# Registers in the middle of each chunk of keys, and 156 score columns for the maxima instead of 228

## What is computed

```python
x = x + attention(group_norm(x))      # 12 heads of 32, window 7 x 7 on a canvas of 48 x 48
x = x + expert_mlp(group_norm(x))     # 4 experts, the best 2 of them

# attention, for every query pixel q of an image and every head:
k_cat = concat([k, reg_k]); v_cat = concat([v, reg_v])   # 48*48 pixels and 16 registers
scores = (q . k_cat) / sqrt(32)
scores = where(in the 7 x 7 window around q (clipped to the canvas) or a register, scores, -1e30)
o = softmax(scores) @ v_cat
```

## Time and profile before

| what | us |
|---|---|
| median of 3 runs | 680.63 |
| lowest and highest | 676.43, 681.11 |
| the profiled execution, its own time | 682.01 |
| its span in the trace | 680.2 |

### The profile page before, as it was taken

One profiled execution on the slowest core, in us unless ns is written; L12 is line 12 of the kernel. 1 busy time (PEld: TensorE's weight loads), 2 busy tenths in 40 slices (PEclk: granted clock), 3 DMA queues, 4 the chain that ended last, 5 costly groups with the idle time before them and its releaser, 6 DMA issues.

```text
span 680.2 us, 22432 instructions
## 1 busy us (share of the span) xinstructions
PE 591.2 (87%) x9235; PEld 413.0 (61%) x9235; DVE 475.6 (70%) x1030; ACT 303.2 (45%) x598; POOL 285.0 (42%) x425
## 2 busy tenths in 40 slices
PE   3578778999799987998899988988878888997997
PEld 2336656677666766567675766757656454564554
DVE  4786465788787889876667868876798875772332
ACT  0663345314554277513562255441774527544231
POOL 4106588235232564436892452224646112212231
PEclk9979689999999999999999999998998998997999
DMA  8959584797419952398518954199530010110112
GB/s 296 177 128 279 168 215 123 192 238 204 118 31 232 274 152 73 84 237 235 145 51 199 250 175 136 37 248 242 164 92 22 1 36 35 56 51 35 71 44 97
DMA packets 131806, 95.94 MB, mean 141 GB/s; under 512 B 67437, under 2 KB 125481, under 8 KB 131705
## 3 DMA queue, kind: packets, MB, share of 16 engines
q1 hardware_dynamic: 121960, 75.18, 43.3%
q0 software_dynamic: 9744, 19.33, 9.1%
HBM read 58.11 MB, written 35.54 MB: 138 GB/s over the span
## 4 chain that ended last, share of the span: by engine, by line
PE 51%; DVE 17%; DMA 11%; SPq 9%; ACT 5%; issue 5%; POOL 2%; ACTq 0%; DVEq 0%; POOLq 0%
PE ps L1041 38%; SPq L270 6%; DVE MX L549 5%; PE ps L1200 4%; DMA KB<-kscr 4%; PE ps L1151 4%; DMA WR<-in_wqkv 2%; DMA vscr<-VT 2%; PE ps L1177 2%; DVE GT_ L481 2%; ACT XH L807 1%; SPq L253 1%; DMA VR<-vscr 1%; DVE SUMT L562 1%; DMA kscr<-KT 1%
## 5 line engine op out<-in xcount | busy, mean ns | idle before, releaser
L549 DVE TENSOR_REDUCE MX<-ps 128x2 f32<-128x456 f32 x216 | 125.4, 626 | 56.4 <-PE ps L1151 55.4
L1041 PE MATMUL ps<-XH,WQ 128*128 128x384 f16 x810 | 146.5, 337 | 9.3 <-DVE XH L491 8.0
L1041 PEld LDWEIGHTS ps<-XH,WQ 128*128 128x128 f16 x810 | 79.8, 101 | 68.2 <-issue 15.2
L866 ACT ACTIVATE PT<-ps 128x448 f32<-128x448 f32 (+1 forms) x162 | 78.7, 511 | 62.6 <-PE ps L1177 62.0
L1151 PE MATMUL ps<-KB,QS 120*32 120x228 f16 x1728 | 66.2, 270 | 29.9 <-DMA KB<-kscr 11.9
L425 POOL TENSOR_TENSOR KT<-QS,KT 128x384 f16<-128x384 f32 x36 | 32.7, 919 | 110.1 <-ACT KT L955 110.1
L1177 PE MATMUL ps<-QS,KB 122*128 122x112 f16 (+1 forms) x864 | 64.5, 215 | 10.2 <-ACT PT L866 5.6
L1041 PE MATMUL ps<-WQ,XH 128*128 128x128 f16 x972 | 63.2, 224 | 2.6 <-issue 2.1
L372 POOL DMA_DIRECT2D QS<-MT x72 | 38.2, 534 | 63.9 <-ACT MT L856 63.8
L1200 PE MATMUL ps<-PT,VR 128*32 128x112 f32 (+1 forms) x1296 | 61.1, 262 | 2.8 <-DMA VR<-vscr 2.8
L1151 PEld LDWEIGHTS ps<-KB,QS 120*32 120x32 f16 x1728 | 34.6, 97 | 47.4 <-DVE MX L549 17.4
(11 more groups left out here) (169 smaller groups left out, 1010.0 us busy)
## 6 DMA issues: line engine op xcount, KB each, us to landing
KB<-kscr SPq DMA_DIRECT2D x108, 192.0 KB, 7.5
kscr<-KT SPq DMA_DIRECT2D x72, 192.0 KB, 2.5
VR<-vscr SPq DMA_DIRECT2D x216, 56.0 KB
QS<-qscr SPq DMA_DIRECT2D x108, 96.0 KB, 6.8
out<-X SPq DMA_DIRECT2D x12, 576.0 KB, 3.3
X<-in_x SPq DMA_DIRECT2D x6, 576.0 KB, 8.2
qscr<-QT POOLq DMA_DIRECT2D x18, 192.0 KB, 3.5
qscr<-PT POOLq DMA_DIRECT2D x18, 192.0 KB, 5.1
```

The source lines that it names most:

```text
L549: V.tensor_reduce(out=MX[:, s % 2, t, 2 * pair:2 * pair + 2], in_=ps[:, S_BANK(s, i), 0:2 * RUN].rearrange("p (h n) -> p h n", h=2), op=AL ...
L866: A(PTS[n % 4][:, 0:w], ps[:, ST_BANK(n), 0:w], ACT.Exp, scale=SCORE).then_inc(s_["exd"], 1)
L1041: last = mm(bank, lhsT(a, k), rhs(b, k), start=(k == 0 and n == 0), stop=(finish and k == steps - 1 and n == 2))
```

## The change

The 16 registers move from the end of each chunk to its middle: 4 rows of keys (56 columns), 16 registers, 4 rows of keys. A run of 32 queries then needs three rows ahead, four rows, three rows behind and one block of registers, whichever half of the chunk its queries belong to: 42 + 56 + 16 + 42 = 156 columns, starting at the chunk or 56 columns into it. What follows from it:

- the copy of keys into chunks writes two halves of 4 rows with a gap of 16 columns (one more dimension in the access pattern);
- a chunk's values no longer lie on 112 partitions in a row but on 56 and 56 with the registers' 16 between, so each chunk is loaded by two DMAs of 4 rows of pixels;
- the wait ahead of a tile's values is split: the first three chunks wait for the first three steps of tile s - 2 only;
- the key tables follow the new order, the slot keeps its 868 columns, and the matmuls on zeros become 36 of 168 columns.

```diff
-LEAD, TAIL = 3 * KW + REGS, 3 * KW
-SLOTW = LEAD + STRIPS * CHUNK + TAIL
-RUN = LEAD + CHUNK + TAIL
+HALO = 3 * KW
+HALF = 4 * KW
+SLOTW = 2 * HALO + STRIPS * CHUNK + REGS
+RUN = 2 * HALO + HALF + REGS
...
-WARM = 26
+WARM = 36
...
-            return bass.AP(flat.tensor, flat.offset, [list(flat.ap[0]), [CT_, TILES], [PADW, 8], [1, KW]])
+            return bass.AP(flat.tensor, flat.offset, [list(flat.ap[0]), [CT_, TILES], [4 * PADW, 2], [PADW, 4], [1, KW]])
...
-                if 36 * gi + 6 * (s - 1) > 0:
-                    sp.wait_ge(s_["pv"], 36 * gi + 6 * (s - 1))
                 if gi == 0 and s == 0:
                     sp.wait_ge(s_["vpad"], 32)
                 for a in range(STRIPS):
-                    sp.dma_start(VR[0:8 * KW, s % 2, a, :], vscr[8 * a:8 * a + 8, CT_ * s:CT_ * s + KW, :]).then_inc(vr_in[s % 2][a // 3], 16)
+                    if a % 3 == 0:
+                        if 36 * gi + 6 * (s - 2) + a + 3 > 0:
+                            sp.wait_ge(s_["pv"], 36 * gi + 6 * (s - 2) + a + 3)
+                    for half in range(2):
+                        sp.dma_start(VR[half * (HALF + REGS):half * (HALF + REGS) + HALF, s % 2, a, :],
+                                     vscr[8 * a + 4 * half:8 * a + 4 * half + 4, CT_ * s:CT_ * s + KW, :]).then_inc(vr_in[s % 2][a // 3], 16)
...
                 for part in range(2):
-                    last = V.tensor_copy(KT[:, a % 3, part, :, 0:8 * KW].rearrange("p s (r c) -> p s r c", c=KW), windows(a, part))
+                    to = KT[:, a % 3, part, :, :]
+                    parts = bass.AP(to.tensor, to.offset, [list(to.ap[0]), [CHUNK, TILES], [HALF + REGS, 2], [KW, 4], [1, KW]])
+                    last = V.tensor_copy(parts, windows(a, part))
...
                     for j in range(4):
-                        a, q0 = 2 * t + j // 2, s * SN + 128 * t + 32 * j
+                        at, q0 = CHUNK * (2 * t + j // 2) + j % 2 * HALF, s * SN + 128 * t + 32 * j
                         last = mm(ps[32 * j:32 * j + 32, S_BANK(s, i), hh * RUN:(hh + 1) * RUN], QS[0:SROWS, h, q0:q0 + 32],
-                                  KB[0:SROWS, h, slot(s), CHUNK * a:CHUNK * a + RUN], start=True, stop=True)
+                                  KB[0:SROWS, h, slot(s), at:at + RUN], start=True, stop=True)
```

More of the change, by code:

```diff
@@ L252, in keys_in @@
                 for j, part in enumerate((0, 1, 0)):
-                    sp.dma_start(KB[DH * j:DH * (j + 1), :, slot(s), LEAD:LEAD + STRIPS * CHUNK],
+                    sp.dma_start(KB[DH * j:DH * (j + 1), :, slot(s), HALO:HALO + STRIPS * CHUNK],
                                  kscr[part, :, s, :, :].rearrange("(h d) a n -> d h (a n)", d=DH)).then_inc(kb_in[slot(s)], 16)
@@ L327, in _ @@
             nc.gpsimd.memset(KU[:, :, :, :, W + 3:PADW], 0.0).then_inc(s_["pads"], 1)
-            nc.gpsimd.memset(KB[0:96, :, :, 0:LEAD], 0.0).then_inc(s_["pads"], 1)
-            nc.gpsimd.memset(KB[0:96, :, :, SLOTW - TAIL:SLOTW], 0.0).then_inc(s_["pads"], 1)
+            nc.gpsimd.memset(KB[0:96, :, :, 0:HALO], 0.0).then_inc(s_["pads"], 1)
+            nc.gpsimd.memset(KB[0:96, :, :, HALO + STRIPS * CHUNK:SLOTW], 0.0).then_inc(s_["pads"], 1)
             def low_half(n, blk, k):
@@ L342, in register_keys @@
                     for part in range(2):
-                        last = nc.gpsimd.tensor_copy(KT[:, i, part, :, CHUNK - REGS:CHUNK],
+                        last = nc.gpsimd.tensor_copy(KT[:, i, part, :, HALF:HALF + REGS],
                                                      KR[:, part, gi % KC, :].unsqueeze(1).broadcast_to([P, TILES, REGS]))
@@ L365, in register_values @@
                 for i in range(2):
-                    pool.dma_start(VR[P - REGS:P, i, :, :], VRG[:, g * P:(g + 1) * P].unsqueeze(1).broadcast_to([REGS, STRIPS, P])
+                    pool.dma_start(VR[HALF:HALF + REGS, i, :, :], VRG[:, g * P:(g + 1) * P].unsqueeze(1).broadcast_to([REGS, STRIPS, P])
                                    ).then_inc(s_["vreg_in"], 16)
@@ L1176, in key_scores @@
                 for h in range(HEADS):
-                    last = mm(ps[:, ST_BANK(n), h * w:(h + 1) * w], KB[0:TROWS, h, slot(s), LEAD + CHUNK * a:LEAD + CHUNK * (a + 1)],
+                    last = mm(ps[:, ST_BANK(n), h * w:(h + 1) * w], KB[0:TROWS, h, slot(s), HALO + CHUNK * a:HALO + CHUNK * (a + 1)],
                               QS[0:TROWS, h, s * SN + CT_ * q0:s * SN + CT_ * q1], start=True, stop=True)
@@ L1184, in weighted @@
                 if a % 3 == 0:
-                    pe.wait_ge(vr_in[s % 2][a // 3], 144 * gi + 48 * (s // 2 + 1))
+                    pe.wait_ge(vr_in[s % 2][a // 3], 288 * gi + 96 * (s // 2 + 1))
                 if a == 0:
@@ L1205, in _ @@
             for i in range(WARM):
-                mm(ps[0:LEAD, 6, 0:HEADS * LEAD], KB[0:96, 0, 0, 0:LEAD], KB[0:96, :, 0, 0:LEAD], start=True, stop=True)
+                mm(ps[0:HALO, 6, 0:HEADS * HALO], KB[0:96, 0, 0, 0:HALO], KB[0:96, :, 0, 0:HALO], start=True, stop=True)
             pe.wait_ge(s_["g_in"], 16)
@@ L1419, in key_tables @@
     for a in range(STRIPS):
-        at = LEAD + CHUNK * a
+        row = [HALO + CHUNK * a + KW * r + r // 4 * REGS for r in range(8)]
+        registers = slice(row[4] - REGS, row[4])
         for q in range(max(0, 8 * a - 8), min(H, 8 * a + 16)):
@@ L1423, in key_tables @@
                 if first(q, H) <= 8 * a + r < first(q, H) + WIN:
-                    out[:, q % 16, at + KW * r:at + KW * (r + 1)] = 0
+                    out[:, q % 16, row[r]:row[r] + KW] = 0
             if q // 8 == a:
-                out[:, q % 16, at + 8 * KW:at + CHUNK] = 0
+                out[:, q % 16, registers] = 0
         for kind, s in enumerate((0, 2, TILES - 1)):
@@ L1431, in key_tables @@
                     if f <= X0[s] + i < f + WIN:
-                        out[kind, 16 + c, at + i:at + 8 * KW:KW] = 0
-                out[kind, 16 + c, at + 8 * KW:at + CHUNK] = 0
+                        out[kind, 16 + c, [at + i for at in row]] = 0
+                out[kind, 16 + c, registers] = 0
     return out
```

## The result

The changed kernel takes 758.7 us (median, 757.4 to 761.7) where the kernel before takes 680.2: 1.118 times as long, with a 95% interval of 1.113 to 1.123. The forecast was 780, with 760 to 802 as the own range of the forecast case and 665 to 803 as the range of all cases.

A forecast was written before the change was run, and what follows sets the result against it. SyncE's queue of value loads was taken to bound the attention phases: 682.0 + 102.3 for doubled issues - 2.9 for shorter scores = 781.4 profiled, so 780 us; case range 760 to 802, 8-in-10 range 665 to 803.

The forecast's parts named there:

- What bounds the kernel: Attention phases: SyncE's queue, 88% full in stage 1, already sets the phase's end, 4.8 us behind the last issue.
- An issue of 56 partitions costs 648 ns: SyncE's loads of values: a halved load keeps the queue as long as a whole one, 0.695 us with the gap.
- case A: SyncE's queue: an issue stays at 648 ns (0.60 to 0.70 us), giving 760 to 802 us; chance 0.55.
- B: SyncE's queue: an issue gets cheaper, but not by half, giving 690 to 760 us; chance 0.15.
- The phases: Six attention phases: 53.2 us from first issue to start of the last, adding +102.3 us in sum.
- Maxima: VectorE's reductions: 456 to 312 elements, 486 ns each, 30.2 us less in all, worth nothing while waiting for values.
- Score runs: TensorE's score matmuls: 72 of 228 columns fewer, at most 0.097 us a unit, 20.9 us in all.
- The 2.9 us ahead of the loads: TensorE, stages 1 to 5: 6 units of scores before the first load of values save 30 x 0.097 us.
- Copy of keys: 72 copies of keys into chunks: one more dimension changes nothing; at most 24 us if the time doubled.
- The split wait gains nothing: SyncE's wait ahead of values: three chunks may start three steps earlier, but late issues gain nothing by it.
- Rival C: SyncE's queue: an issue costs half or less (below some 0.39 us), giving 657 us; chance 0.20 together with Rival D.
- Rival D: Loads of values: DMA engines become the limit, 0.39 us a load on 4 engines, giving 666 us; within Rival C's 0.20.

## Why the prediction was right, and where its size was off

- *What bounds the kernel: SyncE's queue sets the end of the phase.* Shown, from two sides: halved loads alone cost 12%, and with the transfers kept but issued faster or elsewhere the loss shrinks; with the second queue it is gone from the phases of stages 1 and 4.
- *An issue of 56 partitions costs 648 ns.* The step that was off. It is the term of the sum that was mis-sized: 597 ns. By the prediction's own rate of 4.3 us for each 0.01 us, 0.051 are 22 us, and 780 less 22 is 758: the measured 758.7. That 597 ns lies just below case A's lower end of 0.60 us and 758.7 just below its 760, so by the prediction's own bounds the result fell at the upper edge of B. That the corrected sum meets the measurement to 1 us is partly luck: two smaller terms cancel, as the next point shows. The choice of the nearest row held; the reason given for it (time for one instruction of this form) is what the other forms show, with a small part that does follow the size.
- *The phases.* From first to last issue 53.2 us were forecast and 49.7 to 52.4 measured; with 0.645 for 0.695 the same formula gives 71 x 0.645 + 3.8 = 49.6. Over six phases, with the 2.3 for the extra transfers, that is 300 us, and 304.5 were measured: 4 us more. From the last issue to the start of the last matmul of values the six phases have 21.0 us, where the forecast keeps some 25: 4 us less. In stage 1 the last load landed 2.5 us after its issue began, not 3.4. Of the slack that the sum takes off in stages 2 and 5, stage 0 had 1.6 us too (the same matmuls end there at 118.2, the queue alone allowed 116.6), which it leaves out.
- *Maxima.* 486 ns forecast, 477 measured, and worth nothing here, as said.
- *Score runs.* At most 0.097 us less a unit. Measured 58.1 us busy for 66.2 is 0.037 less, and 0.060 in the kernel with registers at the end; part of the changed kernel's runs were at the lower clock (last section). The 2.9 us ahead of the loads: from the last matmul of values to the next stage's first load the five stretches shrank by 3.9 us in sum, 2.5 of them in the last one. That is the size forecast, but no run shows that it comes from the scores; and from that load to the first matmul of values 3.8 us were lost again.
- *Copy of keys.* Median 335 ns before and after, so the further dimension is free.
- *The split wait gains nothing.* Right, to 0.3 us (759.0 with one wait).
- *Rival C's price was too high.* With the loads whole, the queue no fuller than before and the runs short, 657 was forecast and 672 measured. The 21 us for six phases counted savings on TensorE and behind the last wait as if nothing else stood beside them; VectorE's wait for scores grew instead. So with an issue at half its cost I would now expect about 1% of gain, not 3.5, an estimate from the 672.8 and 672.3 us of whole loads; that wasn't run. The nearest run is the one with loads of one form, with a mean issue of 0.46 us and some 0.05 of gap: B's way of adding gives +17 us for it, and it was 22 us slower than its runs of before (699.8 for 678.2).
- *Rival D, the DMA engines.* They weren't the limit, as said: a mean share of 0.27 in the phase of stage 1 (last section) and of 0.17 from 205 to 210, inside its last 36 loads, and landings 2.9, 2.5 and 2.5 us after the issue in the rows shown for this stretch. A mean over 16 engines would hide four that are full; a backlog on those four would show as later and later landings. The page has the same packets in the hardware queue in both kernels, 121,960, though 216 more transfers run in one. If a transfer ends with one small packet on each engine that it uses, equal sums mean half as many engines for each half load. That fits the rule of the Trainium skill (DMA: Bandwidth & Descriptors, Why a DMA increments its semaphore by 16 and not by 1) that the prediction names: 8 engines before, 4 after. Two more kernels agree with it. With loads of 56 rows on both sides the rule gives 14 engines, ten more for each of 432 loads, and the page has 126,280 packets, 4,320 more, all of them under 512 bytes (71,756 for 67,436). The 40 loads behind the kernel's end move 3,064 pieces and have 4 x 92 engines by the rule, 3,432 together; the page has 125,392 packets, 3,432 more. It remains an inference from counts; no run here shows the engines one by one.

## What to carry to other kernels

Before splitting a transfer, multiply the new number of issues by the duration that one issue has in the profile and set it beside the length of the phase and the waits that the queue still has; here an issue cost nearly the same for half the data (597 ns for 647). If a layout needs the split, look for the same saving in the order that keeps the transfer whole: here other bounds of the run and other masks gave it. Before giving loads to a second queue, see in every stage, and between the stages, what its engine does there already.

## What the runs showed of the hardware that I had not expected

The cost of an issue hangs on whether the two sides have the same form: 385 ns for 56 partitions from a list of 56 rows, 612 from 4 rows of 14 pixels, 518 for 64 partitions from 4 rows of 16. When SyncE issued at the faster rate, 31 of 432 issues took over 900 ns.

TensorE's granted clock fell inside the longer phases. Stretches of the changed kernel (PE, PEld, DVE, ACT, POOL busy, clock, DMA share, GB/s): the phase of stage 1, the projections behind it, the phases of stages 2 and 4.

```profile
171.60:218.40 46.80, 34.65 (x858) 27.25 (x858) 25.75 (x63) 18.01 (x40) 7.65 (x11) 0.82 0.27 70
218.40:264.20 45.80, 43.51 (x539) 30.47 (x538) 31.32 (x79) 17.08 (x33) 19.82 (x38) 1.00 0.82 203
264.20:312.90 48.70, 31.01 (x844) 23.60 (x836) 31.57 (x67) 27.68 (x58) 19.14 (x25) 0.92 0.27 70
...
452.50:501.50 49.00, 35.10 (x846) 27.49 (x846) 26.85 (x63) 18.97 (x41) 8.12 (x11) 0.80 0.28 79
```

In the kernel before the phase of stage 1 had 1.00, with TensorE busy for 28.16 of 32.40 us:

```profile
163.60:196.00 32.40, 28.16 (x864) 22.80 (x857) 27.53 (x60) 18.62 (x42) 8.91 (x15) 1.00 0.41 106
```

A mean of 0.82 means part of the phase at the lower of the clock's two levels, 1.2 GHz, and the rest at 2.4. It fits that TensorE is busy for longer in the changed kernel (606.3 us for 591.2) with fewer columns to compute. I take the lower clock to follow the waiting for values and not to cause the loss: the phase's length is explained by the issues alone, and the phase of stage 2, at 0.92, is no shorter than that of stage 1, at 0.82 (47.2 and 45.5 us by the matmuls of `weighted`). No run held the clock fixed to show it.
